# Preparing the feed-forward input inside the local attention layer, with the softmax scaling on GpSimd

## What is computed

```python
def _layernorm(x, axis=-1, eps=1e-05):
    m = jnp.mean(x, axis=axis, keepdims=True)
    v = jnp.var(x, axis=axis, keepdims=True)
    return (x - m) / jnp.sqrt(v + eps)

def fp4_quant_dequant(x):                      # blocks of 16 along the last dimension
    xb = x.reshape(shape[:-1] + (shape[-1] // BLOCK, BLOCK))
    scale = jnp.max(jnp.abs(xb), axis=-1, keepdims=True) / 6.0
    scale = jnp.maximum(scale, jnp.float32(1e-12))
    xn = xb / scale
    idx = jnp.searchsorted(_MID, jnp.abs(xn))
    return (_GRID[idx] * jnp.sign(xn) * scale).reshape(shape)

x = x + _L0_xattn_ref(_layernorm(x), ctx_768, ...)
# local layer: softmax over the last 256 positions, out @ Wout
x = x + _L0_attn_ref(_layernorm(x), Wqkv, Wout)
# feed-forward: silu(xq @ Wgate) * (xq @ Wup), quantised again, @ Wdown
x = x + _L0_ffn_ref(_layernorm(x), w_gate, w_up, w_down)
```

## Time and profile before

| | |
|---|---|
| median of 3 runs | 1454.45 us (1454.37 to 1458.25) |
| profiled execution | 1455.47 us; span of its instructions 1453.5 us |
| TensorE matmul busy | 1353.5 us (93%) |
| VectorE busy | 1143.6 us (79%) |
| ScalarE busy | 814.0 us (56%) |
| GpSimd busy | 786.8 us (54%) |

### The profile page before, as it was taken

One profiled execution on the slowest core, in us unless ns is written; L12 is line 12 of the kernel. 1 busy time (PEld: TensorE's weight loads), 2 busy tenths in 40 slices (PEclk: granted clock), 3 DMA queues, 4 the chain that ended last, 5 costly groups with the idle time before them and its releaser, 6 DMA issues. The chain is left out here.

```text
span 1453.5 us, 39397 instructions
## 1 busy us (share of the span) xinstructions
PE 1353.5 (93%) x16766; PEld 721.0 (50%) x16766; DVE 1143.6 (79%) x1834; ACT 814.0 (56%) x1531; POOL 786.8 (54%) x307
## 2 busy tenths in 40 slices
PE   7988879788899999999999999999999999887798
PEld 4443434344465555555555555545554445556444
DVE  7676777767788888888888888888886764676797
ACT  4443444334477777777777776777677722573212
POOL 3211211212499889898988998899888002000111
PEclk8999999899999999999999999999999999999999
DMA  7556765475615121222122212221210030870000
GB/s 237 171 158 185 209 197 157 156 219 177 189 38 179 61 65 38 65 64 66 37 66 64 66 37 66 64 66 37 66 55 28 5 137 0 176 151 1 1 8 22
DMA packets 127790, 137.44 MB, mean 95 GB/s; under 512 B 44992, under 2 KB 108992, under 8 KB 125696
## 3 DMA queue, kind: packets, MB, share of 16 engines
q1 hardware_dynamic: 127616, 134.93, 31.8%
HBM read 75.66 MB, written 44.17 MB: 82 GB/s over the span
## 5 line engine op out<-in xcount | busy, mean ns | idle before, releaser
L1274 DVE TENSOR_REDUCE early<-attend_banks 128x1 f32<-128x512 f32 x952 | 612.7, 685 | 82.1 <-PE attend_banks L1020 77.0
L1238 ACT ACTIVATE attend_prob<-attend_banks 128x512 f32<-128x512 f32 x1024 | 535.9, 599 | 201.8 <-PE attend_banks L1057 199.6
L1418 POOL TENSOR_TENSOR early<-early,attend_prob 128x1024 f32<-128x1024 f32 x210 | 614.3, 2925 | 37.7 <-ACT attend_prob L1238 9.6
L1057 PE MATMUL attend_banks<-early,k_first 97*32 97x512 f16 x2560 | 263.2, 383 | 3.1 <-ACT attend_prob L1238 3.1
L1020 PE MATMUL attend_banks<-k_first,early 96*32 96x512 f16 x2272 | 235.2, 383 | 1.1 <-PEq L282 1.1
L1020 PE MATMUL attend_banks<-attend_k_rest,early 96*32 96x512 f16 x1536 | 158.7, 380 | 0.0
L1057 PE MATMUL attend_banks<-early,attend_k_rest 97*32 97x512 f16 x1536 | 152.9, 380 | 2.8 <-ACT attend_prob L1238 2.8
L1081 PE MATMUL attend_banks<-attend_prob,ones 128*32 128x128 f32 x3048 | 134.9, 272 | 3.6 <-DVE attend_recip L1286 3.6
L489 POOL TENSOR_TENSOR project_w_whole<-project_grid,project_qscale 128x704 f32<-128x704 f32 x24 | 33.3, 1386 | 189.6 <-DVE project_grid L619 189.6
L1070 PE MATMUL attend_banks<-attend_prob,wkv_area 128*32 128x512 f32 x1024 | 135.0, 592 | 0.0
L1070 PE MATMUL attend_banks<-attend_prob,attend_vh_odd 128*32 128x512 f32 x1024 | 133.3, 592 | 0.0
(11 more groups left out here) (191 smaller groups left out, 1874.9 us busy)
## 6 DMA issues: line engine op xcount, KB each, us to landing
v_scratch<-project_v SPq DMA_DIRECT2D x16, 1024.0 KB, 5.7
early<-in_ctx_dram SPq DMA_DIRECT2D x16, 768.0 KB, 7.1
k_first<-k_scratch SPq DMA_DIRECT2D x36, 256.0 KB, 3.4
k_scratch<-project_k_hi SPq DMA_DIRECT2D x64, 128.0 KB, 2.8
k_scratch<-project_k_lo SPq DMA_DIRECT2D x64, 128.0 KB, 3.0
attend_vh_odd<-v_scratch SPq DMA_DIRECT2D x8, 1024.0 KB, 4.8
wkv_area<-v_scratch SPq DMA_DIRECT2D x7, 1024.0 KB, 4.9
attend_k_rest<-k_scratch SPq DMA_DIRECT2D x24, 256.0 KB, 3.5
```

Of the source, the lines that this page charges most:

```text
L1057: last = nc.tensor.matmul(s_ps[c * HD:(c + 1) * HD, s_bank[n], :], key_rows[:, c * HD:(c + 1) * HD], q_stack[0:KROWS + 1, h, :], start=Tru ...
L1238: nc.scalar.activation(prob[:, q % PSLOTS, t, :], s_ps[:, s_bank[BT * q + t]], ACT.Exp, scale=SCALE).then_inc(p_ready, 1)
L1274: nc.vector.tensor_reduce(part_max[:, s, j, part:part + 1], pre_ps[:, bank], AX.X, ALU.max).then_inc(pre_read, 1)
L1418: nc.gpsimd.tensor_tensor(sums, sums, prob[:, q % PSLOTS, 0:n], ALU.add).then_inc(pool_summed, 1)
```

## The change

It does four things.

1. The preparation of a tile of the feed-forward input (statistics, layer norm, quantisation) becomes a generator `prepare_x` that hands control back after each of its 22 steps. In the local layer, tiles 0 to 2 are prepared by VectorE after their addition: up to four steps at the end of each turn of the loop over units. The last tile is prepared in the feed-forward layer, between the second and the third hidden piece of tile 0.
2. The inverse square root is no longer ScalarE's root and one Newton step for all tiles, but on VectorE alone, a tile at a time: a shift of the bits, a multiplication, a reciprocal and three Newton steps, each on a single column.
3. The probabilities of the local layer are scaled by GpSimd, two multiplications a unit with the inverse sums broadcast over the keys. VectorE keeps the reciprocals; its wait for the scaling is now for three units back.
4. `keep_busy` at the start of the feed-forward layer has 8 matmuls instead of 56.

```diff
+        def quantize(chain, src, dst, n, ready):
...
+            chain.link(nc.vector.tensor_reduce(amax[:, 0:nb], blocks(src), AX.X, ALU.max, apply_absolute_value=True))
+            yield
+            chain.link(nc.vector.tensor_scalar(qscale[:, 0:nb], amax[:, 0:nb], 1.0 / 6.0, 1e-12, ALU.mult, ALU.max))
+            yield
...
+            nc.vector.tensor_tensor(blocks(dst), blocks(qn[:, 0:n]), each(qscale), ALU.mult).then_inc(ready, 1)
...
+        def prepare_x(dve, chain, t):
+
+            one = slice(t, t + 1)
+            chain.link(nc.vector.bn_stats(stats[:, t, :], x[:, t, :]))
+            yield
+            chain.link(nc.vector.bn_aggr(mv[:, t, :], stats[:, t, :]))
+            yield
+            chain.link(nc.vector.tensor_scalar(ve[:, one], mv[:, t, 1:2], EPS, None, ALU.add))
+            yield
+            chain.link(nc.vector.tensor_scalar(r0[:, one].bitcast(U32), ve[:, one].bitcast(U32), 1, None,
+                                               ALU.logical_shift_right))
+            chain.link(nc.vector.tensor_scalar(r1[:, one], r0[:, one], ROOT, None, ALU.mult))
+            yield
+            chain.link(nc.vector.reciprocal(r2[:, one], r1[:, one]))
+            for _ in range(3):
+                yield
+                chain.link(nc.vector.tensor_tensor(r1[:, one], r2[:, one], r2[:, one], ALU.mult))
+                chain.link(nc.vector.tensor_tensor(r0[:, one], r1[:, one], ve[:, one], ALU.mult))
+                yield
+                chain.link(nc.vector.tensor_scalar(r1[:, one], r0[:, one], -0.5, 1.5, ALU.mult, ALU.add))
+                chain.link(nc.vector.tensor_tensor(r2[:, one], r2[:, one], r1[:, one], ALU.mult))
+            yield
+            chain.link(nc.vector.tensor_scalar(xn_f[:], x[:, t, :], mv[:, t, 0:1], r2[:, one], ALU.subtract, ALU.mult))
+            yield
+            yield from quantize(chain, xn_f[:], xq[:, t * D:(t + 1) * D], D, xq_ready)
+            dve.wait_ge(xq_ready, t + 1)
...
+                for n, (t, h) in enumerate(units):
+                    pool.wait_ge(inv_ready, n + 1)
+                    for b in range(2):
+                        some = pr[:, n % 3, b, 0:used(n)].rearrange("p (j w) -> p j w", j=per_bank[t])
+                        first = h + b * per_bank[t]
+                        scales = inv[:, t % 2, first:first + per_bank[t]].unsqueeze(2)
+                        nc.gpsimd.tensor_tensor(some, some, scales.to_broadcast([P, per_bank[t], seen[t][1] * P]),
+                                                ALU.mult).then_inc(p_scaled, per_bank[t])
...
-                def normalise(n):
+                def invert(n):
                     t, h = units[n]
                     dve.wait_ge(p_ready, upto[n])
-                    if n >= 1:
-                        dve.wait_ge(p_scaled, upto[n - 1])
+                    if n >= 3:
+                        dve.wait_ge(p_scaled, upto[n - 3])
                     nc.vector.reciprocal(inv[:, t % 2, h:h + heads[n]], total[:, t % 2, h:h + heads[n]]).then_inc(inv_ready, 1)
-                    dve.wait_ge(inv_ready, n + 1)
-                    for j in range(heads[n]):
-                        b, col = place(n, j)
-                        w = seen[t][1] * P
-                        nc.vector.tensor_scalar(pr[:, n % 3, b, col:col + w], pr[:, n % 3, b, col:col + w],
-                                                inv[:, t % 2, h + j:h + j + 1], None, ALU.mult).then_inc(p_scaled, 1)
...
+                def tiles_of_x():
+
+                    for t in range(TT - 1):
                         dve.wait_ge(y_added, t + 1)
-                        chain(nc.vector.bn_stats(stats[:, t, :], x[:, t, :]))
-
+                        for _ in prepare_x(dve, chain, t):
+                            yield False
+                        yield True
+
+                preparing, added, prepared = tiles_of_x(), 0, 0
+                AT_ONCE = 4
                 for n in range(len(units) + 6):
                     if n < len(units):
                         maxima(n)
                     if 1 <= n <= len(units):
-                        normalise(n - 1)
+                        invert(n - 1)
                     if n - 4 in closes:
                         out_low(closes[n - 4])
                     if n - 6 in closes:
                         add(closes[n - 6])
+                        added = min(closes[n - 6] + 1, TT - 1)
+                    for _ in range(AT_ONCE):
+                        if prepared < added:
+                            prepared += next(preparing)
...
             def _(act):
-                layer_norm_scalar(act, var_ready, sd_ready, 3)
...
-                quantize_x(0)
-                quantize_x(1)
                 for t in range(TT):
                     for c in range(3):
                         quantize_h(t, c)
-                    if t + 2 < TT:
-                        quantize_x(t + 2)
+                        if t == 0 and c == 1:
+                            for _ in prepare_x(dve, chain, TT - 1):
+                                pass
...
-                keep_busy(y_ps[:, 1], 56)
+                keep_busy(y_ps[:, 1], 8)
```

More of the change, by code:

```diff
@@ L1441, in perceiver, with blocks, each @@
         w_rows.append(wq_dram[2][:].rearrange("s p (r c) -> s (p r) c", c=INNER))
+        piece = carve(late)
+        xnT = piece([2, DK, T], F16)
+        oT = piece([2, G, T], F16)
+        xq = piece([TT * D])
+        xn_f = piece([D])
+        NQ = 512
+        qn = piece([NQ])
+        qr = piece([NQ])
+        amax = piece([NQ // QB])
+        qscale = piece([NQ // QB])
+        qinv = piece([NQ // QB])
+        xq_ready = sem_in(whole)("xq_ready")
+        def quantize(chain, src, dst, n, ready):
+            def blocks(ap):
+                return ap.rearrange("p (b e) -> p b e", e=QB)
+            nb = n // QB
+            def each(s):
+                return s[:, 0:nb].unsqueeze(2).to_broadcast([P, nb, QB])
+            chain.link(nc.vector.tensor_reduce(amax[:, 0:nb], blocks(src), AX.X, ALU.max, apply_absolute_value=True))
+            yield
+            chain.link(nc.vector.tensor_scalar(qscale[:, 0:nb], amax[:, 0:nb], 1.0 / 6.0, 1e-12, ALU.mult, ALU.max))
+            yield
+            chain.link(nc.vector.reciprocal(qinv[:, 0:nb], qscale[:, 0:nb]))
+            yield
+            chain.link(nc.vector.tensor_scalar(qinv[:, 0:nb], qinv[:, 0:nb], BELOW, None, ALU.mult))
+            yield
+            chain.link(nc.vector.tensor_tensor(blocks(qn[:, 0:n]), blocks(src), each(qinv), ALU.mult))
+            yield
+            chain.link(nc.vector.tensor_scalar(qr[:, 0:n].bitcast(U32), qn[:, 0:n].bitcast(U32), EXPONENT, None,
+                                               ALU.bitwise_and))
+            yield
+            chain.link(nc.vector.tensor_scalar(qr[:, 0:n], qr[:, 0:n], 1.0, ROUND, ALU.max, ALU.mult))
+            yield
+            chain.link(nc.vector.tensor_tensor(qn[:, 0:n], qn[:, 0:n], qr[:, 0:n], ALU.add))
+            yield
+            chain.link(nc.vector.tensor_tensor(qn[:, 0:n], qn[:, 0:n], qr[:, 0:n], ALU.subtract))
+            yield
+            nc.vector.tensor_tensor(blocks(dst), blocks(qn[:, 0:n]), each(qscale), ALU.mult).then_inc(ready, 1)
@@ L1961, in quantize_h @@
                         dve.wait_ge(w_turned, number[("h", t - 2, c)] + 1)
[L1962 removed]
+                    for _ in quantize(chain, h[:, 0:hi - lo], hq[:, t % 2, lo:hi], hi - lo, hq_ready):
+                        pass
                     dve.wait_ge(hq_ready, n + 1)
```

48 lines of the change are left out of this document (10 added, 38 removed).

## The result

| | before | after |
|---|---|---|
| median of the runs | 1454.41 us (1451.12 to 1458.25, 4 runs) | 1472.76 us (1470.89 to 1476.54, 4 runs) |
| span of the profiled execution | 1453.5 us | 1474.7 us |
| ratio, 95% interval | | 1.0129 (1.0096 to 1.0161) |

The changed kernel is slower by 18.4 us; 11.6 were forecast, and 1472.76 lies outside the 1462 to 1470 that the forecast gave for itself. To see where, both traces are cut at the same three points: the start of the first maxima (VectorE's TENSOR_REDUCE into `local_top`), the end of the last addition of the local layer, and TensorE's first filling matmul of the feed-forward layer.

What follows compares the result with a forecast made beforehand. With the steps VectorE was to become the local layer's chain: 1455.5 us profiled + 14.0 local + 4.7 holds - 6.9 feed-forward = 1467.3, the median 1.0 lower, so 1466. By itself 1462 to 1470; wide range 1454 to 1473.

Steps and rivals of the forecast that it cites:

- the chain: Local layer, tile 0's addition to the last reciprocal: VectorE sets the pace, its work and waits summing to 49.9 us.
- Front and GpSimd's multiplication: Local loop: tile 0's addition 1.5 us later (0 to 3); a GpSimd multiplication 0.91 us, 1.9 us a unit.
- the holds: Local loop: GpSimd holds one VectorE operation by 0.67 us in every second of 14 turns, 4.7 us.
- VectorE's waits: Local layer: four waits of 1.70 us at two tile closings, for ScalarE's copy and the next scores, 6.8 us.
- The tail: End of the local layer, last scaling to last addition: 7.8 us as before, with GpSimd's 1.9 ahead of it.
- the 9.4: Local loop: the holds if one VectorE operation is held in each of 14 turns, 9.4 us.
- (b): Local loop: one held operation every turn, 9.4 us, TensorE's clock possibly lower on top; 1471 us, chance 0.15.
- The feed-forward layer: Last stage: gain 2.2 + 4.7 = 6.9 us; 9.4 if the clock doesn't fall, 5.9 with one more us of holds.
- the standstill: Feed-forward layer, TensorE's second piece of tile 1: it waits 8 to 10 us for a product behind tile 3's preparation.
- (a): Local loop: GpSimd and VectorE don't hold each other, the 4.7 us falls away; 1461.6 us, chance 0.20.
- (c): Local loop: steps fill the closings' waits; local layer grows by 7, feed-forward gives 7 back; 1454.5 us, chance 0.10.
- (d): Local loop: VectorE's slack takes all steps, local layer keeps its length; 1447.6 us, 1445 at full clock, chance 0.10.

Runs made afterwards that it cites:

- the filled kernel: The changed kernel with filling matmuls in all TensorE pauses (local loop, tail, ahead of the first gate matmul, long standstill), against the kernel before: 1465.06 us, ratio 1.0049.
- the repeat: The changed kernel, local code unaltered, with tile 3's preparation moved one tile later in the feed-forward layer, against the kernel before: 1472.6 us, ratio 1.0112.

## Why the prediction was right or wrong

The direction was right, by the mechanism that was named: the steps made VectorE the chain from tile 0's addition to the last reciprocal. The size was too small: the time lies above the 1462 to 1470 of the forecast itself and inside the wide range of 1454 to 1473, just under its end. By the steps:

**Front and GpSimd's multiplication.** Tile 0's addition came 0.7 us later, 1.5 was taken. A pair of 384 columns took 1.61 us unheld, so 0.80 each (0.91 taken, bounds 0.76 and 0.95); the broadcast operand is the nearer row.

**The chain.** 54.6 us were forecast with the holds (49.9 + 4.7), 58.8 measured. Term by term, each instruction counted to the start of the next: the steps without holds 24.3 as summed (24.6); maxima, reciprocals and closings 16.1 instead of 18.5, since the next instruction starts before a maximum or a reciprocal has ended (at 1290.23 a maximum lasts 0.96 us and the reciprocal starts 0.87 later); the holds 9.5 instead of 4.7; VectorE's waits 8.8 instead of 6.8. -0.3 - 2.4 + 4.8 + 2.0 = +4.1, 4.2 before rounding. The tail came to 11.65 instead of 9.7, and the front to 0.8 less: 18.7 + 4.2 + 1.9 - 0.8 = 24.0. So two terms that were too small stand against one that was too large by 2.4, and the miss looks smaller than it is.

**The first step that failed: the holds.** "One in every second turn", with single columns unseen, was mis-sized: 4.7 us taken, 9.5 measured. The products of a single column are held like whole tiles, 11 of the 27. The sentence from the Trainium skill (GPSIMD Engine Reference, 1. Specifications) that the engines contend when VectorE reads two SBUF tensors is borne out here: the products with two inputs took 356 to 449 ns on average, the same products with one input and a scalar 214 ns and never longer. It was set aside for 4.7 and pointed to the 9.4. That 9.5 was measured is in part luck: the 9.4 is one hold of 0.67 in each of 14 turns, the trace has 6.4 us on products, mostly two in a turn and none in others, and 3.1 us on six other lines. And the price of the product holds in time is not their length: taking them away gave 4.0 to 4.7 us with the clock low, and 0.5 us of local part with TensorE at full clock.

**The second: TensorE's clock in the loop has no term in the sum.** It stood only as an aside in rival (b). Behind tile 0's addition the loop had a full clock before; the change lengthens TensorE's pauses to as much as 2.9 us, and the mean clock of 0.85 there makes transposes, values and back-projections slower, which lie in the same ring. This is in the waits and the tail above, and the filled kernel prices it: 6.9 us of the 24.0 (6.2 against the repeat), and rather more, since the filling costs time too. With the clock held full, the local part was +17.1 where 18.7 were forecast, with held products still in it (10 of the 27). That is the larger cause of the miss. A sum over VectorE's durations can't contain it, since it sits in TensorE's durations, which the sum took as unchanged.

**The feed-forward layer.** -6.9 forecast, -6.2 measured; the standstill of 9.53 us was forecast as 8 to 10, at the right product, the clock behind it fell as said, and the first gate matmul came 4.9 us into the stage where about 5 were forecast. The alternative figure of 9.4 for a clock that doesn't fall was met by the two kernels filled everywhere, -9.5 and -8.8.

**The rivals.** (a) falls by the held rows. That the time without product holds and at full clock, 1462.65, is near its 1461.6 says nothing for it: that kernel has the other holds and a filled TensorE. (b) had the right size of holds and named the clock; its 1471 is the nearest. (c) and (d) fall: the waits at a closing stayed (1.72 and 2.79 us where 1.70 and 1.70 were), and nothing went into them. The run with tile 0 alone shows how near (d) was for a third of the work: one step a turn cost 0.8 us up to tile 2's addition.

Open is how the 6.9 us split into single pauses and how much more the low clock costs than filling gives back. In the loop GpSimd's way by itself cost 3.8 us at a full clock; in the tail it can't be told from the filling.

## What to carry to other kernels

Steps that are put behind each turn of a ring are paid as soon as their engine becomes the chain (20.1 us for three tiles); put in only what the next stage needs first, and at a rate below the slack of one turn (0.8 us for one step a turn). When a change makes TensorE's pauses longer, give the clock a term of its own and price it by a group of matmuls that the trace shows at both levels; filling matmuls get it back only where they fit into the pause, and cost time where they don't. Before work on GpSimd is put beside small VectorE work, look which of its operations the trace shows held; for products of single columns the form with a scalar per partition wasn't.

## What the runs showed of the hardware

- A VectorE product of two single columns was held by GpSimd like a large one: 128x1 took 0.83 and 0.75 us beside two multiplications of 0.80, and 11 of 27 such products were held, 6.4 us in all. A tensor_scalar of one column with its scalar from memory took 0.21 us and was not held in any of 27 in either of two kernels, but costs 0.05 more than the product by itself (0.16).
- One input alone doesn't protect: a tensor_scalar on 128x32 (L1473) took 459 ns on average in the change and 182 with GpSimd idle, one on 128x512 integers (L1477) 596 and 427.
- TensorE's clock fell in a loop in which no single wait of TensorE was longer than 2.9 us: 0.80 and 0.84 on average from 1289 to 1359, with 0.99 in 1305 to 1313 and 0.58 in the 8 us behind. The same twelve matmuls took 2.76 us at full clock and 4.28 to 5.09 at or near the lower level.
- Five filling matmuls (1.33 us) ahead of each wait kept the clock at 1.00 in the change without any other edit; in the kernel with GpSimd's scaling alone, which had a full clock anyway, they made the chain 7.5 us longer.
- GpSimd multiplied 128x384 with a broadcast factor in 0.80 us and 128x512 in 1.02 to 1.03.
